# Unread products on TensorE at the end of the front stage, and three ahead of each pair of the first maxima

## The reference

```python
h = _layernorm(x) * (1 + ca) + sa
qkv = h @ qkv_w.T + qkv_b            # 16 heads of 16 features, q and k rotated (rope)
attn = softmax(einsum('bhnd,bhmd->bhnm', q, k) * scale)
x = x + ga * (einsum('bhnm,bhmd->bhnd', attn, v) @ proj_w.T + proj_b)
h = _layernorm(x) * (1 + cb) + sb
x = x + gb * ffn(h)                  # each token goes to the expert of 8 that its gate picks
```

## Time and profile before

| | |
|---|---|
| median of 3 runs | 1914.36 us (1913.94 to 1916.68) |
| the profiled execution, its own time | 1919.9 us |
| span of its records | 1918.2 us |
| TensorE busy | 1810.2 us, 94% |
| VectorE busy | 1663.7 us, 87% |
| ScalarE busy | 1419.5 us, 74% |
| mean granted clock of TensorE | 0.952 |
| `front` | 0 to 139 us |
| ahead of the attention's loop | 139 to 200 us |

### The profile page before, as it was taken

One profiled execution on the slowest core, in us unless ns is written; L12 is line 12 of the kernel. 1 busy time (PEld: TensorE's weight loads), 2 busy tenths in 40 slices (PEclk: granted clock), 3 DMA queues, 4 the chain that ended last, 5 costly groups with the idle time before them and its releaser, 6 DMA issues. The chain is left out here.

```text
span 1918.2 us, 38667 instructions
## 1 busy us (share of the span) xinstructions
PE 1810.2 (94%) x15410; PEld 908.2 (47%) x15410; DVE 1663.7 (87%) x1797; ACT 1419.5 (74%) x2642; POOL 573.8 (30%) x412
## 2 busy tenths in 40 slices
PE   7976999999999999999999999999999984999996
PEld 4542333333333333333333333333333374999996
DVE  6769699999999999999999999999996574888885
ACT  1330688888888888888888888888888631877774
POOL 1115311151225115113311621421182025344442
PEclk8985699999999999999999999999999985999998
DMA  5765011241141233115114211511114553888872
GB/s 192 231 158 130 1 71 47 70 90 47 47 102 60 68 65 75 47 65 97 63 53 77 62 58 60 108 53 47 48 50 159 180 186 114 270 273 265 266 239 61
DMA packets 143428, 208.84 MB, mean 109 GB/s; under 512 B 42954, under 2 KB 88557, under 8 KB 141456
## 3 DMA queue, kind: packets, MB, share of 16 engines
q1 hardware_dynamic: 130992, 179.18, 32.4%
q0 software_dynamic: 7904, 18.80, 3.6%
q10 hardware_dynamic: 4352, 8.39, 1.2%
HBM read 123.15 MB, written 73.45 MB: 102 GB/s over the span
## 5 line engine op out<-in xcount | busy, mean ns | idle before, releaser
L1244 DVE TENSOR_REDUCE att_mx<-att_PM 128x2 f32<-128x1024 f32 x1024 | 1245.5, 1225 | 77.8 <-PE att_PM L1101 71.1
L1212 ACT ACTIVATE att_probs<-att_PS 128x512 f32<-128x512 f32 x2048 | 1112.6, 596 | 197.9 <-PE att_PS L1088 160.1
L1134 PE MATMUL att_PV<-att_probs,att_VU 128*32 128x256 f32 x8192 | 659.2, 394 | 7.7 <-ACT keep_sums L1233 6.2
L1088 PE MATMUL att_PS<-att_QE,K 50*128 50x512 f32 x2048 | 537.2, 500 | 2.0 <-ACT att_probs L1212 1.8
L1101 PE MATMUL att_PM<-K,QM 50*128 50x512 f32 x2048 | 441.1, 415 | 21.9 <-DVE att_mx L1244 15.0
L1088 PEld LDWEIGHTS att_PS<-att_QE,K 50*128 50x128 f32 x2048 | 204.0, 185 | 436.7 <-ACT att_probs L1212 413.7
L1134 PEld LDWEIGHTS att_PV<-att_probs,att_VU 128*32 128x32 f32 x8192 | 163.0, 108 | 371.1 <-issue 205.4
L978 POOL CAST att_mh<-att_m 128x16 fp32r<-128x16 f32 x32 | 6.3, 198 | 814.5 <-DVE att_m L1251 814.5
L1101 PEld LDWEIGHTS att_PM<-K,QM 50*128 50x128 f32 x2048 | 207.4, 192 | 44.4 <-DVE att_mx L1244 36.5
L575 POOL TENSOR_TENSOR QM<-QS,QM 16x1024 fp32r<-16x1024 f32 x62 | 146.6, 2365 | 8.5 <-POOL QM L994 6.1
L566 POOL TENSOR_TENSOR K<-KS,K 16x4096 fp32r<-16x4096 f32 x14 | 125.2, 8942 | 1.8 <-POOL K L1005 1.3
(11 more groups left out here) (212 smaller groups left out, 1645.0 us busy)
## 6 DMA issues: line engine op xcount, KB each, us to landing
H<-in_w SPq DMA_DIRECT2D x44, 1024.0 KB
routed_rows<-att_filling SPq DMA_DIRECT2D x32, 1088.0 KB, 4.3
att_QE<-QM SPq DMA_DIRECT2D x32, 512.0 KB, 3.0
QS<-qkT SPq DMA_DIRECT2D x186, 64.0 KB, 2.4
KS<-qkT SPq DMA_DIRECT2D x42, 256.0 KB, 9.1
qkT<-KS ACTq DMA_DIRECT2D x16, 512.0 KB, 5.3
all_X<-routed_rows SPq DMA_DIRECT2D x23, 258.0 KB
all_X<-in_x SPq DMA_DIRECT2D x4, 1024.0 KB, 9.9
```

Of the source, the lines that this page charges most:

```text
L1088: nc.tensor.matmul(PS[score_bank(i)][:], K[r % BODY // CHUNKS][rows, ab, kt * P:(kt + 1) * P], QE[r % 2][rows, ab, :], start=True, stop=Tr ...
L1134: last = nc.tensor.matmul(PV[32 * h:32 * h + VW, cols], VU[r // CHUNKS % 2][:, j, h, :], probs[:, j % SLOTS, h, cols], start=j == 0 and ha ...
L1212: nc.scalar.activation(probs[:, kt % SLOTS, h, :], PS[score_bank(i)][:], ACT.Exp).then_inc(exps, 1)
L1244: nc.vector.reduce_max(mx[:, r % 2, at:at + 2, kc], PM[bank][:], AX).then_inc(maxima, 1)
```

## The change

At the end of `front`, TensorE issues four more products of 128x128 weights and 512 columns into the first bank of `psq`, after it has waited for a copy of the last round. Nothing reads them. In `attention`, a new function `repeat` issues products of the same kind as those of `pair_product`, with the keys of unit 0 and the queries of the step given, into the three score banks `PS`, on the row halves 0, 64 and 0. Nothing reads these either. Three of them stand ahead of the wait of each maximum pair of the prologue, save the first pair of either stretch.

```diff
--- before.py
+++ after.py
@@ -543,6 +543,9 @@
                             last = nc.tensor.matmul(psx[:, b, 0:D], bvb[:, k, b, :], wp[:, k, :],
                                                     start=k == 0, stop=k == KD - 1)
                     last.then_inc(x_products, 1)
+            pe.wait_ge(qk_copied, 4 * ROUND - 3)
+            for n in range(4):
+                nc.tensor.matmul(psq[:, 0, 0, :], wf[B - 1][:, 0, 0:P], xT[(ROUND - 1) % 2][:, 0, :], start=True, stop=True)
 
 
 def load_keys(eng, g, stage, unit, done):
@@ -1102,6 +1105,15 @@
                                             K[u][rows, ab, kc * CH:(kc + 1) * CH], start=True, stop=True)
                 last.then_inc(max_products, 1)
 
+            def repeat(r, n, times):
+
+
+                qt, ab, kc = n // 8, n // 4 % 2, n % 4
+                for i in range(times):
+                    rows = slice(64 * (i % 2), 64 * (i % 2) + ROWS)
+                    nc.tensor.matmul(PS[i % SBANKS][:], QM[r][rows, ab, qt * P:(qt + 1) * P],
+                                     K[0][rows, ab, kc * CH:(kc + 1) * CH], start=True, stop=True)
+
             def next_pair(s, r, it, last, at, ahead, n):
 
                 shift = shift_at(r, last)
@@ -1156,11 +1168,15 @@
 
             pe.sem_inc(pv_groups, SLOTS)
             for n in range(PAIR_TILES):
+                if n:
+                    repeat(0, n, 3)
                 pe.wait_ge(maxima, n - 1 + AHEAD)
                 pair_product(n % 2, 0, 0, n)
             pe.wait_ge(ident_set, 3)
             turn_shifts(0, PAIR_TILES % 2, PAIR_TILES)
             for n in range(2 * EARLY):
+                if n:
+                    repeat(1, n, 3)
                 if n == 1:
                     pe.wait_ge(shifts_out, 1)
                 else:
```

## The result

The changed kernel takes 1919.6 us (median of 20 executions, 1913.99 to 1925.14), the kernel before, beside it on the same chips, 1913.12 us (20 executions, 1908.02 to 1919.23). The ratio is 1.0039 with a 95% interval of 1.0029 to 1.0049: slower by 7.5 us, 5.5 to 9.4 (the two medians lie 6.5 us apart). The forecast was 1915.3 and "same". The time lies in the range, but only because the range was drawn wide enough to take in the rival on the slower side (1920.8), and it is that rival, held for 0.22, that came true; the stretch that the prediction called "same" ends at 1918.2.

A forecast was written before the change was run, and what follows sets the result against it. It took VectorE to bound the 46 maximum pairs and half-clock TensorE the loop's first 12 rounds. The sum 0 + 1.3 - 0.4 + 0 = +0.9 us on the median 1914.36 gave 1915.3 us, range 1903.5 to 1922.

The forecast's parts named there:

- same: Whole kernel: a time of 1910.5 to 1918.2 us, not told from no change; chance 0.48.
- the rival on the slower side: Maximum pairs: clock does not return, TensorE bounds all 44 pairs with repeats, +6.5 us, 1920.8; chance 0.22.
- Front products, cost 0: End of front stage: four products take 3.5 us, end at 136.0, before the next stage begins at 139.46.
- The price of a slot: Maximum pairs: 0.43 us per slot at half clock, three 1.28 against VectorE's 1.134, so 0.147 us a pair.
- The far bound of 0.64 a pair: Maximum pairs: a start of its own for every slot gives 1.77 us a pair, 28 us in all, 1942; 1 in 20.
- How many pairs run at half clock: Maximum pairs: clock returns 4 to 7 us after the first; five slow pairs, then four, 9 x 0.147 = 1.3 us.
- the sum of 0.9 us: All steps: 0 for front products, +1.3 for slow pairs, -0.4 at the scores, 0 in the loop.
- The start of the scores, -0.4: First scores: with the clock whole at 194, the first score comes 2 x (0.43 - 0.21) = 0.4 us sooner.
- The loop, gain 0: Steady loop: clock falls again at 196 to 200, so the loop starts at half clock as before.
- How long the loop stays slow: Steady loop: TensorE, starting at half clock, needs the same 26 us or so until the clock returns.
- all that the change can win: Steady loop: 12 rounds at half clock, 2.16 against 1.24 us each, 11.0 us.
- The median against the profiled run: Whole kernel: the 5.5 us between profiled 1919.9 and median 1914.36 is untouched by the change, so the sum adds to the median.

The follow-up runs named there:

- front_only: The changed kernel without its repeats, leaving only the four front products; 1907.58 us, ratio 1.0005 to the kernel before.
- full_rows: The changed kernel with two repeats ahead of each pair instead of three, each on all 128 rows; 1936.5 us, ratio 1.0167 to the kernel before.
- turn_burst: Kernel before plus 16 all-row products while shifts are turned, then two all-row repeats per pair and all-row products around the first exponentials; 1902.14 us, ratio 0.9973.
- turn_half: turn_burst with its 16 products on rows 0 to 49 instead of all 128; one execution, 1921.6 us beside 1913.7 for the kernel before.
- burst_full: The changed kernel plus 24 products in a row on all 128 rows between the first and second pair; one execution, 1913.9 us.
- pairs_only: The changed kernel without its four front products, leaving the repeats alone; 1911.14 us, ratio 1.0042 to the kernel before.
- two_repeats: The changed kernel with two repeats ahead of each pair instead of three, on row halves 0 and 64; 1904.65 us, ratio 0.9996 to the kernel before.
- burst_half: The changed kernel plus 24 products in a row on rows 0 to 49 between the first and second pair; one execution, 1922.5 us.
- front_seven: The changed kernel with seven front products instead of four; 1911.21 us, ratio 1.0032 to the kernel before.
- held: front_seven plus 12 all-row products while shifts are turned and 50-row products among the first scores; 1911.85 us, ratio 1.0039 to the kernel before.
- held_full: Changed kernel with eight front products, all-row repeats (six, then two per pair), and all-row fillers at turned shifts and first scores; 1900.43 us, ratio 0.9968.

## Why the prediction was right and wrong

- *Front products, cost 0*: right. They run from 132.28 for 3.60 us (forecast 3.5), the idle time after them is 3.17 (forecast 3.5), and front_only shows no cost (1.0005, 0.9996 to 1.0014).
- *The price of a slot*: right. 0.43 us at half clock, 1.28 a pair, 0.147 over VectorE. The far bound of 0.64 a pair, for a start of its own per product, did not come in the change, but full_rows met its like: 1.88 us a pair, 0.74 over VectorE, where the number of rows changes between products.
- *How many pairs run at half clock*: this is the step that failed. I expected 9 and it was all 44, 44 x 0.147 = 6.5 us; the reductions took 6.52 more. I had read the return at 115 to 125 as the work of products "without a gap", and carried it to repeats without a gap. The products of the earlier trace rows were on 128 rows. The changed kernel's products filled 1.28 us of each 1.28, two of the three slots with products on both halves, 100 rows together, and the clock stayed at 0.50. turn_burst and turn_half part the two: equally gapless, the products on 128 rows bring the clock back and those on 50 do not. The evidence stood in my own rival, that the loop ran for 26 us with no gap and slow; I gave it 0.22 where it deserved the most. That the time lies in the range is therefore luck as far as this step goes: the sum of 0.9 us was not what happened.
- *The start of the scores, -0.4*: not there, since the clock was not whole. From the end of the last reduction to the loop's value products 5.33 us, before 5.19. The 0.21 us in this sum is half of 0.43 and stands in no row; the same prediction takes 0.34 for a slot at full clock elsewhere. In burst_full 24 products on all rows took 5.75 us at full clock, 0.24 each.
- *The loop, gain 0*: right in size, for another reason. I had the clock whole at 194 and falling at 196 to 200; it was never back.
- *How long the loop stays slow*: I took 26 us as fixed. It is not. After the loop's first value products the clock returned 26.8 us later in the profiled execution of before, and 13.7 in that of after. With the same loop it was 16.1 in front_only, 5.1 in pairs_only, 26.8 in two_repeats, 7.2 in full_rows, 13.9 in burst_full, 20.3 in burst_half, 20.4 in front_seven and 5.2 in held: over the ten profiles a median of 15.0. At 0.92 / 2.16 saved for each slow microsecond (by the 2.16 and 1.24 us of a round), the spread from 5.1 to 26.8 is worth 9 us; executions of before, and of after, spread by 11.2 us. The times do go with the clock: in after the fastest execution has a mean granted clock of 0.958 and the slowest 0.951, which is some 28 us more at half clock. That the loop's start is where they lie is shown for the profiled executions alone, and it is not the whole spread, since turn_burst, whose profiled loop starts whole, still spreads by 6.5 us in 12 executions (the kernel before by 16.6 in 23 beside it). So the 11.0 us that I called "all that the change can win" was at the upper end of what one execution shows; at 15.0 us slow it is 6.4. The versions that have the whole clock in the loop win 5 to 6 us in the median: held_full -0.0032 x 1906.3 = -6.1, with 1.5 us lost at the stage end, where the first reduction waits 4.41 us and not 2.92; turn_burst -0.0027 x 1906.3 = -5.1, with 1.7 us lost at the turned shifts, where it waits 4.59 and not 2.86.
- *The median against the profiled run*: I added the sum to 1914.36 and said that the 5.5 us to the profiled 1919.9 lie in and around that execution. Its loop was slow for 26.8 us; against the median of 15.0 this is worth 11.8 x 0.92 / 2.16 = 5.0 us, an estimate that would account for nearly all of it. A comparison of the two profiles misleads for the same reason: in after the loop's slow part is short by luck (which gives back 5.6 of the 6.3 us: 13.1 x 0.92 / 2.16), and later, at 1435.9 to 1446.2, a slow spell that before does not have costs 10.3 x 0.92 / 2.16 = 4.4 us. The three together give 6.3 - 5.6 + 4.4 = 5.1 us of the 5.2 between the two spans, so that difference is near the cost only by accident. The cost itself rests on the ratio (7.5 us, 5.5 to 9.4) and on the +6.5 us of the reductions, which agree.

The Trainium skill, in TensorE: Matmul & The Clock Gate, section What's actually happening, says that activity releases the throttle. These traces agree with it for unbroken runs of products on all 128 rows (held at 179.8, turn_burst at 178.5), and show that a TensorE which is busy in every record is not thereby active in that sense: 40.88 us without a gap at 0.50.

What stays open: what the clock goes by. Rows read is what was varied; the runs do not part it from anything that changes along with the rows. They do not tell whether it was the pairs on 50 rows or the late starts that kept full_rows at half clock; nor why the loop, the same instructions each time, is released after 5 us in one execution and after 27 in another, or what began the slow spell at 1435.9.

## What to carry to other kernels

Filler products must be of a shape that the trace has shown to bring the full clock back; here that is all 128 rows, one after another (mixed with pairs on 50 rows they did not do it in full_rows), and the narrow shape of the real work was not enough however densely it was issued. Price fillers at half clock against the engine that bounds the stretch, with the change of shape between products in it, because that is what is paid if the clock does not come: two slots of one shape were free, three cost 6.5 us, and three with changes of shape cost 30. A burst on all rows (turn_burst) inside an idle time that exists anyway, just ahead of the stretch where TensorE is the bound, was the sturdiest form (1899.1 to 1905.6 in 12 executions).

## What was not expected of the hardware

- The same 16 products of 512 columns brought the clock back on 128 rows and left it at 0.50 on 50 rows (turn_burst and turn_half).
- At full clock, TensorE at work for 0.96 of each 1.13 us on 50 rows lost it, some 7 us after the repeats began in burst_full (143.57 to 150.4) and 5 us in held (181.43 to 186.7).
- A change between products on 50 rows and on 128 rows costs 0.30 us at half clock; at full clock three slots with two changes took 1.09 us in held_full (from 142.81 to 143.90), just inside VectorE's 1.134.
- The loop's slow start ends anywhere from 5.1 to 26.8 us after its first value products, and this is worth up to 9 us of an execution's time.
